# An attention block with post-norm and a quantized feed-forward: one tile's normalization epilogue is issued one tile later

## What is computed

```python
def attn(x, w_qkv, w_fc, b_fc, gamma, beta):
    qkv = einsum('bsd,ed->bse', x, w_qkv)
    q, k, v = split(qkv, 3, axis=-1)
    att = softmax(einsum('bqd,bkd->bqk', q, k) * DIM**-0.5, axis=-1)
    y = einsum('bqk,bvd->bqd', att, v)          # k and v are summed apart
    y = einsum('bqd,ed->bqe', y, w_fc) + b_fc
    h = x + y
    return (h - mean(h)) * rsqrt(var(h) + 1e-5) * gamma + beta
def ffn(x, w1, conv_w, conv_b, w2):
    h = bit_linear(x, w1)                       # int8 rows, ternary weights
    h = silu(depthwise_conv1d(h) + conv_b)
    return bit_linear(h, w2)
x = layernorm(x + attn(x, ...))
x = layernorm(x + ffn(x, ...))
```

## Time and profile before

| | us |
|---|---|
| runs of the kernel | 4987.86 and 5054.03, median 5020.95 |
| the profiled execution | 4985.56 |
| its span on the slowest core (core 5) | 4983.8 |
| spans of the 8 cores in it | 4968.0 to 4983.8 |
| first stage A3 in it, first matmul to last store issued | 520.6 to 1015.0 |
| second stage A3 in it | 1336.5 to 1830.1 |

### The profile page before, as it was taken

The page is one execution under the profiler, slowest core; times in us unless marked ns, Lnnn a source line. Parts: engine busy times, 40 slices in busy tenths (PEclk is TensorE's granted clock), DMA queues, the critical chain, the costliest instruction groups (busy, mean ns, idle before and its releaser), DMA issues. The chain is left out here.

```text
span 4983.8 us, 35107 instructions; the slowest of 8 cores (4968.0 to 4983.8 us)
## 1 busy us (share of the span) xinstructions
PE 1824.9 (37%) x8500; PEld 922.2 (19%) x8500; DVE 3281.4 (66%) x4522; ACT 967.7 (19%) x1773; POOL 25.7 (1%) x52
## 2 busy tenths in 40 slices
PE   0046323217422312323233332333323333106999
PEld 0022111103111101212122211121111221102444
DVE  3213577712377767888888888888888888874333
ACT  2200122200011212222232222222222222200111
POOL 0000000000000000000000000000000000000000
PEclk9998766658866656665666666666565756558999
DMA  5521111131211122000000000000000000035443
GB/s 167 147 36 46 64 43 42 38 57 17 81 46 43 44 74 96 6 23 23 23 19 5 23 23 23 21 3 23 23 23 23 3 20 17 17 114 169 150 155 106
DMA packets 189264, 258.95 MB, mean 52 GB/s; under 512 B 63490, under 2 KB 131330, under 8 KB 187012
## 3 DMA queue, kind: packets, MB, share of 16 engines
q1 hardware_dynamic: 163716, 197.95, 13.1%
q10 hardware_dynamic: 18432, 41.97, 2.5%
q0 software_dynamic: 6912, 16.78, 2.1%
HBM read 188.47 MB, written 75.52 MB: 53 GB/s over the span
## 5 line engine op out<-in xcount | busy, mean ns | idle before, releaser
L855 PE MATMUL ps_a<-xqF,tw 128*128 128x258 bf16 (+1 forms) x1024 | 218.7, 385 | 986.4 <-DVE ubuf L866 775.4
L587 PE MATMUL ps_s<-kf,qf 128*128 128x512 bf16 x1024 | 290.2, 453 | 609.9 <-ACT disc L604 607.5
L879 ACT ACTIVATE vt<-ubuf,cbcol,cwcol 128x256 f32<-128x256 f32 x512 | 307.7, 601 | 920.5 <-DVE ubuf L866 891.2
L855 PE MATMUL ps_s<-xqF,tw 128*128 128x258 bf16 (+1 forms) x2048 | 319.1, 311 | 51.8 <-DVE ubuf L866 49.7
L803 DVE TENSOR_TENSOR accb<-accb,rbuf 128x2048 bf16<-128x2048 bf16 x256 | 313.6, 1225 | 19.7 <-issue 0.9
L855 PEld LDWEIGHTS ps_a<-xqF,tw 128*128 128x128 bf16 x1024 | 125.0, 130 | 1064.2 <-issue 1022.0
L743 DVE SCALAR_TENSOR_TENSOR vt<-ubuf,cwcol,vt 128x256 f32<-128x256 f32 x512 | 248.3, 485 | 84.5 <-issue 54.9
L750 DVE SCALAR_TENSOR_TENSOR vt<-ubuf,cwcol,vt 128x256 f32<-128x256 f32 x512 | 248.2, 485 | 40.4 <-issue 2.6
L1018 PE MATMUL ps_c<-tw,hq 128*128 128x512 bf16 x512 | 195.7, 382 | 201.0 <-DMA hq<-hqs 201.0
L758 ACT ACTIVATE ubuf<-vt 128x256 f32<-128x256 f32 x512 | 213.8, 417 | 270.5 <-DVE vt L750 253.5
L587 PEld LDWEIGHTS ps_s<-kf,qf 128*128 128x128 bf16 x1024 | 113.0, 113 | 787.7 <-issue 711.6
(11 more groups left out here) (137 smaller groups left out, 3057.1 us busy)
## 6 DMA issues: line engine op xcount, KB each, us to landing
hqs<-hqst SPq DMA_DIRECT2D x16, 2048.0 KB, 8.8
wstage<-w1T SPq DMA_DIRECT2D x8, 2048.0 KB, 10.3
wstage<-w2T SPq DMA_DIRECT2D x32, 512.0 KB, 4.0
xres<-x_tm SPq DMA_DIRECT2D x32, 512.0 KB, 3.3
x1s<-x1t ACTq DMA_DIRECT2D x32, 512.0 KB, 9.6
qstage<-w1T SPq DMA_DIRECT2D x8, 2048.0 KB, 8.5
qstage<-w2T SPq DMA_DIRECT2D x32, 512.0 KB, 3.3
xres<-x1s SPq DMA_DIRECT2D x32, 512.0 KB, 8.0
```

Of the source, the lines that this page charges most:

```text
L587: t.matmul(ps_s[kb][:, 0:KBW], qf[:, dc * S + qcol: dc * S + qcol + 128], kf[:, dc * S + kb * KBW: dc * S + (kb + 1) * KBW], start=(dc == ...
L855: lo=lo, hi=hi, w0=w0, W=W: t.matmul(bank[:, 0:W], tw[:, dc * H + hc * 128: dc * H + hc * 128 + 128], xqF[:, (par * DC + dc) * WW + (lo - w0):
L879: p.op("scalar", lambda sc, hc=hc: sc.activation(out=vt1[:, (hc % 4) * T1W2:(hc % 4) * T1W2 + T1], in_=ubuf[:, hc * T1W2 + 1:hc * T1W2 + 1 ...
```

## The change

`emit_epilogue` is called for tile qt-1 inside the iteration of tile qt, after the exponentials of tile qt have been appended and before the wait for them; the last tile's epilogue follows the loop. The dictionaries `mm_at` and `epi_q` keep what the call needs from its own tile: the count of `mm`, the row, the parity, the semaphores and the count of stores to wait for. `emit_epilogue` itself, the buffers and everything outside A3 are the same.

```diff
@@ -570,6 +570,8 @@
                 p = PB(nc, f"A3_{s_i}")
                 dO_bases = {0: dO.n, 1: dOb.n}
                 exp_ev = {}
+                mm_at = {}
+                epi_q = {}
                 for qt in range(NGRP * NQT):
                     row0 = s_i * S + qt * 128
                     qcol = qt * 128
@@ -590,6 +592,7 @@
                                      kf[:, dc * S + kb * KBW: dc * S + (kb + 1) * KBW],
                                      start=(dc == 0), stop=(dc == DC - 1)),
                                  inc=(mm if kb == KB - 1 and dc == DC - 1 else None))
+                    mm_at[qt] = mm.n
                     p.wait("vector", mm, mm.n)
                     for kb in range(KB):
                         p.op("vector", lambda v, kb=kb: v.reduce_max(
@@ -607,6 +610,12 @@
                             accum_out=colsb[:, 16 + kb:17 + kb]),
                             inc=(ssm if kb == KB - 1 else None))
                     exp_ev[qt] = ssm.n
+                    if qt >= 1:
+                        row0p, parp, stop, depp, ldp = epi_q[qt - 1]
+                        ev = emit_epilogue(p, row0p, None, None, mm_at[qt - 1],
+                                           eb, "attn", parp, dep_store=depp,
+                                           sto=stop, ldsem=ldp)
+                        ev_h2_list.append(ev)
                     p.wait("vector", ssm, exp_ev[qt])
                     p.op("vector", lambda v: v.reduce_sum(
                         out=colsb[:, 24:25], in_=colsb[:, 16:16 + KB], axis=AX.X))
@@ -623,9 +632,13 @@
                     dep = dO_bases[par] + (48 * (qt // 2) if qt >= 2 else 0)
                     if qt == 0:
                         ev_h2_list = []
-                    ev = emit_epilogue(p, row0, None, None, mm.n, eb, "attn",
-                                       par, dep_store=dep, sto=sto, ldsem=ldsem)
-                    ev_h2_list.append(ev)
+                    epi_q[qt] = (row0, par, sto, dep, ldsem)
+                qt_last = NGRP * NQT - 1
+                row0p, parp, stop, depp, ldp = epi_q[qt_last]
+                ev = emit_epilogue(p, row0p, None, None, mm_at[qt_last], eb,
+                                   "attn", parp, dep_store=depp, sto=stop,
+                                   ldsem=ldp)
+                ev_h2_list.append(ev)
                 p.run()
         p = PB(nc, f"A3drain_{s_i}")
         for eng in ("sync", "scalar", "vector", "tensor", "gpsimd"):
```

## The result

The changed kernel takes 4924.73 us (median of 11 runs, 4920.5 to 4988.1); the kernel before, beside it, 4997.59 us (median of 10 runs). The ratio is 0.983 with a 95% interval of 0.979 to 0.988. A second comparison gave 0.986 (0.981 to 0.991). So it is faster, by 1.4 to 1.7%.

The account below looks back on a forecast made before the run. The prediction took each A3 tile as a serial round of DVE work with ACT's 3.3 us exposed and PE hidden; 100.8 - 19.5 - 14.4 = 66.9 us off 4985.56 gave 4919 us, range 4890 to 4990.

Parts of the forecast that it names:

- The wait that goes: DVE's idle time at L611 for ACT's exponentials falls from 3.52 to 0.16 us in 30 tiles, saving 100.8 us.
- The late square: ACT's first square (L298), queued behind four exponentials, starts 0.65 us late and delays DVE's L302; 19.5 us lost in all.
- Filling the pipeline: In tile 1 of each sequence DVE's maxima wait 7.36 us for matmuls instead of 0.16; 14.4 us lost in all.
- Hidden: From tile 2 PE's matmuls keep 11.7 us of cover; the `xres` load and the three stores cost nothing.
- The sum: 100.8 - 19.5 - 14.4 = 66.9 us saved: 4919 us, period 27.6 us, each A3 33.5 us shorter.
- B: Rival: nothing is given back, square not late or with slack, fill covered; all 100.8 us kept, 4885 us; chance 0.07.
- C: Rival: epilogue's first wait or squares hold DVE until the exponentials are through; 4986 us, up to 5000; chance 0.07.
- D: Rival: DVE and ACT slow each other side by side, losing 4.0 us a tile against 3.36 saved; 5018 us; chance 0.06.

Follow-up runs that it names:

- one-bank runs: Kernel before and changed kernel, each with one bank of exponentials instead of four: A3 452.1 us in the order of before, 447.9 us in the changed order.

## Why the prediction was right

**The wait that goes.** Right: 3.52 us fell to 0.16, in 30 tiles, and the one-bank runs show both sides of it, exposed in the old order (40.7 us for 16 x 2.54) and hidden in the new.

**The late square.** Right in kind, with a detail wrong. The prediction put L302 0.65 us late and said that before "it waits for the square, not for L296". The square is 0.70 late (725.11 against 724.41; the gap behind the last exponential is 0.14, not 0.08), but L302 follows its start by 1.25 us, where the earlier trace rows have 1.37. In the old order L302 stood 0.15 behind the end of L296 (813.83 + 1.22 = 815.05, L302 at 815.20): it was the row sum that set it. So the loss is 0.70 - 0.12 = 0.58 us. The idle time in the wait view, 0.73, is this and the old 0.15. That the forecast of 0.65 came so near is in part luck: the square was 0.05 later than forecast, and the 0.12 of slack behind the row sum was left out; the two errors partly cancel.

**Filling the pipeline.** Right: 7.42 us of wait against 7.36 forecast on the slowest core, the group 8.79 against 8.72. Over all cores the wait is 7.61 on average, and the longest group took 10.00 us, at a mean granted clock of 0.70. The slowest core's group had a mean clock of 0.80, near the 0.81 of the earlier trace rows, so part of it ran at each level, and a fully slow group did not occur. That agrees with the rule of the Trainium skill, "TensorE: Matmul & The Clock Gate", section "Part 1: The HAM clock gate", that the throttled state is the default and activity releases it.

**Hidden.** Right: 11.4 us of cover for PE against 11.7 forecast; no wait for stores or for `xres` in the wait view.

**The sum.** 15 x (3.36 - 0.58) - 7.26 = 34.4 us a sequence with the slowest core's wait, 34.3 with the mean one; measured 34.5, forecast 33.5. The period of 27.43 is 0.2 below the forecast: 0.07 is the square, and the rest is scatter of single cores. As a mean over cores and sequences the period fell from 30.27 to 27.47 us, by 2.80, and 3.36 - 0.58 is 2.78. The forecast for the profiled execution was 4919 and it took 4924.73: its slowest core entered A3 7.4 us later than the slowest core before. The prediction named as a sign of being wrong that stages outside A3 change by more than a few us. The 6 and 11 us above are at the edge of that; they stay within what the one-bank run shows of executions in the old order.

**The rivals.** B fell: both costs are there, though the argument against it, that L302 already waited for the square before, was the misreading above. C fell: no idle time at L291 beyond the 0.23 that was there. D fell: L291, L293 and L296 take 1.22 to 1.23 us beside the exponentials, these 0.69, and DVE's busy time over the whole kernel is 3281.7 against 3281.4 us. That agrees with the Trainium skill, "SBUF — State Buffer", section "SBUF: two separate sides", for DVE and ACT with GpSimd idle.

## What to carry to other kernels

To hide the time in which one engine waits for another's answer, put just enough independent work of the waiting engine between question and answer, and choose work that asks nothing of the answering engine. Here 4.9 us of pure DVE work hid 3.4 us of exponentials for nothing, where the whole 22 us epilogue hid them at the price of a late square in each tile and of one exposed group of matmuls in each sequence. Such a fill is paid wherever the deferral begins, and it is avoided by leaving at home the part of the work that covers the slower engine.

## What was not expected of the hardware

An exposed matmul group has no fixed price. In the changed kernel the same 32 matmuls of tile 1, after the same 8.2 us of idle PE, took 8.35 to 10.00 us over the cores and sequences, at mean granted clocks of 0.84 to 0.70. The groups of tiles 1 and 2 of the first sequence on core 7:

```profile
536.36 10.00 PE L589 MATMUL ps_s<-kf,qf 128*128 128x512 bf16 x32 [8.20 <-ACT disc L607]
553.27 8.39 PE L589 MATMUL ps_s<-kf,qf 128*128 128x512 bf16 x32 [6.91 <-ACT disc L607]
```

On core 1 the groups of the same two tiles took 8.79 and 9.47 us after the same idle times, the other way round. The idle time ahead of a group does not tell its length. So a sum for an exposed group needs a range, here 1.7 us wide. Nothing of this is seen while the group is hidden.
